# State-space scan stage of a fused layer: order of the tiles, second norm, softplus and diagonals

## The reference

```
z   = LN(x)                       zn = LN(z) * norm_w + norm_b
p   = zn @ x_proj_w.T             split into rank part r (128), B (64 states), C (64 states)
dt  = softplus(r @ dt_proj_w.T + dt_proj_b)
h_n[t] = exp(-exp(A_log[n]) * dt[t]) * h_n[t-1] + dt[t] * zn[t] * B_n[t]     for 64 states n
y[t]   = sum_n C_n[t] * h_n[t]  +  D_param * z[t]
x  += y @ out_proj_w.T
```

## Time and profile before

| | us |
|---|---|
| three runs | 678.47, 679.4, 685.2 |
| median | 679.4 |
| the profiled execution, its time | 682.74 |
| its span, first to last instruction | 680.9 |
| VectorE busy, whole span | 498.0 |
| scan stage, first statistics to the last sum | 36.19 to 169.03 |
| first scan starts, last scan starts | 67.99, 159.16 |
| mean of one scan, of one product with C | 2.285, 2.756 |
| mean granted clock of TensorE | 0.927 |

### The profile page before, as it was taken

How to read it: one execution, slowest core, us unless ns; L and a number is a source line. 1 busy time by engine, 2 the same in 40 slices (tenths; PEclk the granted TensorE clock), 3 DMA queues, 4 the chain that set the end, 5 groups by cost and what they waited for, 6 DMA issues and landing times. The chain is left out here.

```text
span 680.9 us, 12861 instructions
## 1 busy us (share of the span) xinstructions
PE 583.0 (86%) x4813; PEld 395.7 (58%) x4813; DVE 498.0 (73%) x852; ACT 396.1 (58%) x750; POOL 335.5 (49%) x265
## 2 busy tenths in 40 slices
PE   4976899997899999799953878878788988889997
PEld 3542355444677777587730555545455575668886
DVE  4357999996678885479966999999999945433322
ACT  4226975552435554456775999999899943421111
POOL 1009999996204442244605898998878830000000
PEclk9987999999999999999975898897887769999999
DMA  9526600000927664046547788897859638900000
GB/s 354 237 74 252 247 0 1 0 1 0 310 83 238 212 210 140 17 127 176 149 130 161 147 141 172 156 175 155 162 132 159 122 64 337 398 1 1 0 1 15
DMA packets 97090, 92.90 MB, mean 136 GB/s; under 512 B 70595, under 2 KB 88323, under 8 KB 93638
## 3 DMA queue, kind: packets, MB, share of 16 engines
q1 hardware_dynamic: 93760, 90.46, 47.9%
q10 hardware_dynamic: 3270, 1.65, 0.8%
HBM read 68.59 MB, written 6.62 MB: 110 GB/s over the span
## 5 line engine op out<-in xcount | busy, mean ns | idle before, releaser
L2150 DVE TENSOR_REDUCE d_nmax<-d_psum 128x1 f32<-128x1024 f32 x128 | 151.5, 1212 | 5.2 <-PE d_psum L2306 5.2
L2306 PE MATMUL d_psum<-kst,qT 96*128 96x512 bf16 x256 | 90.7, 452 | 38.2 <-ACT d_e L2247 15.7
L528 POOL TENSOR_TENSOR b_h<-b_h,b_cb 128x1024 f32<-128x1024 f32 x32 | 88.2, 2756 | 6.3 <-DVE b_h L578 4.5
L2247 ACT ACTIVATE d_e<-d_psum,d_nmax 128x1024 f32<-128x1024 f32 x64 | 71.3, 1115 | 14.9 <-DVE d_nmax L2150 14.4
L2130 POOL TENSOR_SCALAR d_rounded<-d_e,d_lift 128x1024 f16<-128x1024 f32 x64 | 72.1, 1127 | 13.8 <-issue 6.8
L2130 POOL TENSOR_SCALAR d_rounded<-spare,d_lift 128x1024 f16<-128x1024 f32 x62 | 70.4, 1135 | 16.0 <-ACT d_lift L2251 11.8
L578 DVE TENSOR_TENSOR_SCAN b_h<-b_dA,b_psum 128x1024 f32<-128x1024 f32 x32 | 73.1, 2285 | 2.5 <-ACT b_dA L633 2.0
L633 ACT ACTIVATE b_dA<-b_dtT,b_A 128x248 f32<-128x248 f32 x128 | 53.7, 490 | 33.1 <-DVE b_h L578 28.1
L2247 ACT ACTIVATE spare<-d_psum,d_nmax 128x1024 f32<-128x1024 f32 x64 | 71.4, 1122 | 1.9 <-DVE d_nmax L2150 1.9
L689 PE MATMUL b_psum<-b_bdiag,b_dtx 128*128 128x512 f32 x128 | 60.2, 594 | 0.8 <-DVE b_h L578 0.8
L2333 PEld LDWEIGHTS d_psum<-d_ident_f,d_rounded 128*128 128x128 f16 x512 | 40.8, 115 | 32.5 <-issue 18.9
(11 more groups left out here) (439 smaller groups left out, 1189.3 us busy)
## 6 DMA issues: line engine op xcount, KB each, us to landing
c_w<-in_w0gu SPq DMA_DIRECT2D x16, 768.0 KB, 4.8
kst<-kT_scratch SPq DMA_DIRECT2D x84, 128.0 KB, 2.7
w<-in_w SPq DMA_DIRECT2D x5, 1920.0 KB, 21.3
b_cb<-c_scratch SPq DMA_DIRECT2D x4, 2048.0 KB, 7.1
c_w<-in_w0dn SPq DMA_DIRECT2D x16, 384.0 KB, 5.6
kT_scratch<-k_kT SPq DMA_DIRECT2D x12, 384.0 KB, 3.7
a_ctx<-in_ctx SPq DMA_DIRECT2D x2, 2048.0 KB, 18.8
k_ctxT<-in_ctxT SPq DMA_DIRECT2D x12, 256.0 KB, 3.1
```

Source lines behind the costliest of these rows:

```text
L528: nc.gpsimd.tensor_tensor(hv, hv, cv, ALU.mult).then_inc(hc_ready, 1)
L2150: nc.vector.tensor_reduce(nm[:, t, m:m + 1, f:f + 1], quarter(m, j).unsqueeze(1), AX.X, ALU.max, negate=True).then_inc(nm_ready, 1)
L2247: nc.scalar.activation(e[j].unsqueeze(1), quarter(m, j).unsqueeze(1), ACT.Exp, bias=nm[:, t, m:m + 1, f], accum_out=zp[:, t, m:m + 1, f]). ...
L2306: last = nc.tensor.matmul(quarter(m, j)[:, b * 512:(b + 1) * 512], qT[0:QROWS, m:m + 1, t * P:(t + 1) * P], kst[m % 2][0:QROWS, at:at + 51 ...
```

## The change

- Norms: `LayerNorm` is split into `moments` and `inverse`. The second norm's variance is worked out from the first's: var(z) = var(x) * rstd * rstd. zn is written from x directly with the product of both factors, and z after it, with a semaphore of its own.
- TensorE transposes zn alone and signals, then z; the 13 fillers there are gone. VectorE makes znT first, without waiting between the halves, and zDT after it.
- Softplus: Exp is written to SBUF, Ln takes 1 + e in its own pass, the relu part runs before Exp is waited for, and the lost part of 1 + e is added as a polynomial in four operations. The reciprocal, the comparison and three products are gone. The 20 fillers become 13, and they run behind the transposes of C.
- dtxT, its transposes and dtx go by channel halves.
- The decays of tiles 0 and 1 wait for dt alone.
- Tiles: for the first 8 groups the halves alternate (m = 2n + c), then groups 8 to 15 of half 0, then those of half 1.
- Diagonals: GpSimd makes those of 20 states, 4 an instruction; ScalarE 88, 4 ahead of the decays and 4 behind the decays of each tile.

```
@@ -81,19 +81,8 @@
...
-        for t in range(TC):
-            last = nc.vector.bn_stats(self.stats[:, t, :], in_[:, t, :])
-        step(last)
-        for t in range(TC):
-            last = nc.vector.bn_aggr(self.mv[:, t, :], self.stats[:, t, :])
-        step(last)
-        nc.vector.tensor_scalar(self.ve[:, :], self.mv[:, :, 1], LN_EPS, None, ALU.add).then_inc(self.var_ready, 1)
-        dve.wait_ge(self.std_ready, 1)
-        step(nc.vector.reciprocal(self.rstd[:, :], self.std[:, :]))
-
-        step(nc.vector.scalar_tensor_tensor(self.std[:, :], self.ve[:, :], -0.5, self.rstd[:, :], ALU.mult, ALU.mult))
-        step(nc.vector.tensor_tensor(self.std[:, :], self.std[:, :], self.rstd[:, :], ALU.mult))
-        step(nc.vector.scalar_tensor_tensor(self.rstd[:, :], self.std[:, :], 1.5, self.rstd[:, :], ALU.add, ALU.mult))
+        self.moments(step, in_)
+        self.inverse(dve, step, self.mv[:, :, 1])
...
@@ -105,6 +94,27 @@
...
+    def moments(self, step, in_):
+
+        nc = self.nc
+        for t in range(TC):
+            last = nc.vector.bn_stats(self.stats[:, t, :], in_[:, t, :])
+        step(last)
+        for t in range(TC):
+            last = nc.vector.bn_aggr(self.mv[:, t, :], self.stats[:, t, :])
+        step(last)
+
+    def inverse(self, dve, step, var):
+
+        nc = self.nc
+        nc.vector.tensor_scalar(self.ve[:, :], var, LN_EPS, None, ALU.add).then_inc(self.var_ready, 1)
+        dve.wait_ge(self.std_ready, 1)
+        step(nc.vector.reciprocal(self.rstd[:, :], self.std[:, :]))
+
+        step(nc.vector.scalar_tensor_tensor(self.std[:, :], self.ve[:, :], -0.5, self.rstd[:, :], ALU.mult, ALU.mult))
+        step(nc.vector.tensor_tensor(self.std[:, :], self.std[:, :], self.rstd[:, :], ALU.mult))
+        step(nc.vector.scalar_tensor_tensor(self.rstd[:, :], self.std[:, :], 1.5, self.rstd[:, :], ALU.add, ALU.mult))
...
@@ -407,9 +417,13 @@
...
-    CHUNK = 2 * NT
-    POOLED = 10 * NT
-    SPARE = 3
+    CHUNK = NT
+    POOLED = 5 * NT
+    SPARE = 4
+    TOGETHER = 8
+    ORDER = [(c, n) for n in range(TOGETHER) for c in range(DCH)] \
+        + [(c, n) for c in range(DCH) for n in range(TOGETHER, TILES)]
+    ENDS = ORDER.index((0, TILES - 1))
...
@@ -431,16 +445,20 @@
...
-        sp_relu, sp_z, sp_r, sp_q = (h[s][:, q * DCH * T:(q + 1) * DCH * T].rearrange("p (c t) -> p c t", c=DCH)
-                                     for s in range(2) for q in range(2))
+        sp_relu, sp_lost, sp_e = (h[q // 2][:, q % 2 * DCH * T:(q % 2 + 1) * DCH * T].rearrange("p (c t) -> p c t", c=DCH)
+                                              for q in range(3))
...
-        sp_e, sp_l, sp_u, sp_d = (ps[:, b, :].rearrange("p (c t) -> p c t", c=DCH) for b in range(4))
+        sp_d, sp_l, sp_c = (ps[:, b, :].rearrange("p (c t) -> p c t", c=DCH) for b in range(3))
+        var_z = sb("b_var_z", [P, TC])
+        scale_zn = sb("b_scale_zn", [P, TC])
...
@@ -451,8 +469,8 @@
...
         def tiles_of(body):
 
-            for m in range(DCH * TILES):
-                body(m // TILES, m % TILES, m, m % UN)
+            for m, (c, n) in enumerate(ORDER):
+                body(c, n, m, m % UN)
...
@@ -531,43 +549,49 @@
...
-                lnA.vector(dve, step, z, x)
-                lnB.vector(dve, step, zn, z)
-                nc.vector.tensor_copy(lnA.std[:, :], lnB.rstd[:, :]).then_inc(zn_ready, 1)
+                lnA.moments(step, x)
+                lnA.inverse(dve, step, lnA.mv[:, :, 1])
+                step(nc.vector.tensor_tensor(var_z[:, :], lnA.mv[:, :, 1], lnA.rstd[:, :], ALU.mult))
+                step(nc.vector.tensor_tensor(var_z[:, :], var_z[:, :], lnA.rstd[:, :], ALU.mult))
+                lnB.inverse(dve, step, var_z[:, :])
+                step(nc.vector.tensor_tensor(scale_zn[:, :], lnA.rstd[:, :], lnB.rstd[:, :], ALU.mult))
+                for out, by, ready in ((zn, scale_zn, zn_ready), (z, lnA.rstd, z_ready)):
+                    for t in range(TC):
+                        nc.vector.tensor_scalar(out[:, t, :], x[:, t, :], lnA.mv[:, t, 0:1], by[:, t:t + 1], ALU.subtract,
+                                                ALU.mult).then_inc(ready, 1)
                 dve.wait_ge(w_in, 80)
+                dve.wait_ge(znT_psum, 1)
+                for k in range(KC):
+                    nc.vector.tensor_scalar(znT[:, k, :], ps[:, 0, k * T:(k + 1) * T], cols[:, 0, k:k + 1],
+                                            cols[:, 1, k:k + 1], ALU.mult, ALU.add).then_inc(znT_ready, 1)
                 dve.wait_ge(zT_psum, 1)
                 for k in range(KC):
-                    step(nc.vector.tensor_scalar(znT[:, k, :], ps[:, 0, k * T:(k + 1) * T], cols[:, 0, k:k + 1],
-                                                 cols[:, 1, k:k + 1], ALU.mult, ALU.add))
                     step(nc.vector.tensor_scalar(zDT[:, k, :], ps[:, 1, k * T:(k + 1) * T], cols[:, 3, k:k + 1],
                                                  None, ALU.mult))
-                nc.vector.tensor_copy(lnA.std[:, :], lnB.rstd[:, :]).then_inc(znT_ready, 1)
...
                 nc.vector.tensor_copy(cT[:, :], ps[0:N, 5, 0:T]).then_inc(cT_ready, 1)
-                dve.wait_ge(spe_ready, DCH)
-                nc.vector.tensor_scalar(sp_u, sp_e, 1.0, None, ALU.add).then_inc(spu_ready, 1)
-                step(nc.vector.tensor_scalar(sp_d, sp_e, 1.0, 1.0, ALU.add, ALU.subtract))
-                step(nc.vector.tensor_scalar(sp_z, sp_d, 0.0, None, ALU.is_equal))
...
-                step(nc.vector.reciprocal(sp_r, sp_d))
+                dve.wait_ge(spa_ready, DCH)
                 for k in range(DCH):
                     step(nc.vector.tensor_scalar(sp_relu[:, k, :], ps[:, 4, k * T:(k + 1) * T], cols[:, 2, k:k + 1], 0.0,
                                                  ALU.add, ALU.max))
+                dve.wait_ge(spe_ready, DCH)
+                step(nc.vector.tensor_scalar(sp_d, sp_e, 1.0, 1.0, ALU.add, ALU.subtract))
+                step(nc.vector.tensor_tensor(sp_lost, sp_e, sp_d, ALU.subtract))
+                step(nc.vector.scalar_tensor_tensor(sp_c, sp_d, -2.0, sp_lost, ALU.add, ALU.mult))
+                step(nc.vector.scalar_tensor_tensor(sp_relu, sp_c, -0.5, sp_relu, ALU.mult, ALU.add))
                 dve.wait_ge(spl_ready, 1)
-                step(nc.vector.tensor_tensor(sp_d, sp_l, sp_r, ALU.mult))
-                step(nc.vector.tensor_tensor(sp_q, sp_d, sp_z, ALU.add))
-                step(nc.vector.tensor_tensor(sp_d, sp_e, sp_q, ALU.mult))
-                nc.vector.tensor_tensor(dtT[:, :, :], sp_d, sp_relu, ALU.add).then_inc(dt_ready, 1)
+                nc.vector.tensor_tensor(dtT[:, :, :], sp_l, sp_relu, ALU.add).then_inc(dt_ready, 1)
                 dve.wait_ge(dt_ready, 1)
-                nc.vector.tensor_tensor(dtxT[:, :, :], dtT[:, :, :], znT[:, :, :], ALU.mult).then_inc(dtxT_ready, 1)
-                dve.wait_ge(dtx_psum, 1)
-                nc.vector.tensor_copy(dtx[:, :, :], ps[:, 6, :].rearrange("p (t c) -> p t c", t=TC)).then_inc(dtx_ready, 1)
-
-
-                dve.wait_ge(dtx_ready, 1)
+                for c in range(DCH):
+                    nc.vector.tensor_tensor(dtxT[:, c, :], dtT[:, c, :], znT[:, c, :], ALU.mult).then_inc(dtxT_ready, 1)
+                for c in range(DCH):
+                    dve.wait_ge(dtx_psum, c + 1)
+                    nc.vector.tensor_copy(dtx[:, :, c * P:(c + 1) * P], ps[:, 6 + c, 0:T].rearrange("p (t c) -> p t c", t=TC))\
+                      .then_inc(dtx_ready, 1)
+                dve.wait_ge(dtx_ready, DCH)
                 nc.vector.tensor_copy(lnA.std[:, :], lnB.rstd[:, :]).then_inc(h_ready, UN)
...
@@ -606,12 +630,13 @@
...
                 for k in range(DCH):
-                    astep(nc.scalar.activation(sp_l[:, k, :], ps[:, 4, k * T:(k + 1) * T], ACT.Abs,
-                                               bias=cols[:, 2, k:k + 1]))
+                    nc.scalar.activation(sp_l[:, k, :], ps[:, 4, k * T:(k + 1) * T], ACT.Abs,
+                                         bias=cols[:, 2, k:k + 1]).then_inc(spa_ready, 1)
+                act.wait_ge(spa_ready, DCH)
                 for k in range(DCH):
                     nc.scalar.activation(sp_e[:, k, :], sp_l[:, k, :], ACT.Exp, scale=-1.0).then_inc(spe_ready, 1)
-                act.wait_ge(spu_ready, 1)
-                nc.scalar.activation(sp_l, sp_u, ACT.Ln).then_inc(spl_ready, 1)
+                act.wait_ge(spe_ready, DCH)
+                nc.scalar.activation(sp_l, sp_e, ACT.Ln, bias=1.0).then_inc(spl_ready, 1)
                 act.preload_act_table(ACT.Exp)
...
@@ -619,14 +644,15 @@
...
-                first = 2 * TC * NT
+                first = 4
...
                 def decay(c, n, m, s):
-                    act.wait_ge(h_ready, m + (UN - 1))
+                    if m >= 2:
+                        act.wait_ge(h_ready, m + (UN - 1))
...
                     for at in late[first + m * SPARE:first + (m + 1) * SPARE]:
                         diagonal(*at)
```

(28 more changed lines are left out.)

9 lines of the change are left out of this document (5 added, 4 removed).

## The result

| | before | after |
|---|---|---|
| median of 20 runs each | 682.53 us | 677.6 us |
| ratio after to before | | 0.9934 (0.9915 to 0.9953) |
| profiled execution, span | 682.74, 680.9 | 679.14, 677.3 |
| mean granted clock | 0.927 | 0.909 |

The change gains 4.9 us, 0.7%. The forecast was 670 with a range from 665 to 675.5. The measured time lies outside it: of the 9.9 us of its sum 4.9 arrived.

The account below looks back on a forecast made before the run. VectorE bounds the scan at 2.94 us per tile, and the serial chain ahead shifts everything. Gains 5.07 + 6.2 + 0.3 less 1.7 for the clock give 9.9 us; from the middle reading, 681.1, that gives 671.2; stated 670, range 665 to 675.5.

Parts of the forecast that it names:

- Norms and transposes: From the first norm's inverse deviation to drT: projection and drT start 5.07 us earlier, 1.85 of it from late fillers.
- Softplus: From drT's start to dt ready: 7.22 us in place of 13.45, a gain of 6.2 us.
- Scan pitch in the steady part: Tiles stay 2.94 us apart, set by VectorE; ScalarE's four diagonals per tile take 1.29 and fit.
- rival 3: Scan tiles: ScalarE becomes the bound with four diagonals, 3.24 us against 2.94 for 21 tiles; 675.8 us, chance 0.08.
- Rival 2: Clock low in more places, doubling the projection and dt matmuls: gain 7.0 us, 672.4 us, chance 0.14.
- Rival 5: Slower: first scan tiles at half clock, each low tile costing 2.7 us; 8 give 689.4 us, chance 0.03.
- rival 1: Before the first scan: no clock fall, or one ending before TensorE has work; gain 11.6 us, 667.8 us, chance 0.15.
- dt to the first scan: From dt ready to scan 0: gain 0.3 us (0 to 0.8), with dtxT's two halves priced at 0.92 together.
- Scan. Alternating halves changes no tile's work: Scan tiles: VectorE keeps 2.94 us per tile, no drive waits for a diagonal; priced at nothing.
- The clock's price: TensorE idles 3 us before dtxT, its clock falls for 3.41 us at half speed: 1.7 us lost (0 to 3.4).
- a half of dtxT over 0.9 (the lock): Sign of being wrong: VectorE and GpSimd lock each other out of SBUF at dtxT; priced up to 1.9 us worse.
- an end that comes earlier by less than the first scan does: Sign of being wrong: the kernel's end gains less than the first scan, forecast 9.9 to 11.6 us earlier.

Follow-up runs that it names:

- l: The kernel before with only the softplus changed (Abs, Exp and Ln on ScalarE, no reciprocal): 688.25 us, ratio to before 1.0075.
- m: k with the norms, transposes and their 13 fillers as before: 675.38 us, ratio to before 0.9878.
- a: The change, with GpSimd's second product with C made to wait for VectorE's first half sum: 678.43 us, ratio to before 0.9922.
- e: The change plus an unread 0.40 us copy on VectorE between scans 0 and 1: 674.89 us, ratio to before 0.9883.
- r: The change plus only k's filler matmuls in TensorE's waits at the stage's end: 679.09 us, ratio to before 0.9926.
- b: The change with 28 filler matmuls in place of 13 behind the transposes of C: 680.35 us, ratio to before 0.9948.
- c: The change, with GpSimd pausing its diagonals until both halves of dtxT are written: 677.22 us, ratio to before 0.9903.
- d: The change with the edits of a, b and c together: 675.99 us, ratio to before 0.9901.
- k: f plus 13 more filler matmuls in TensorE's waits at the stage's end: 670.37 us, ratio to before 0.9806, the fastest kernel.
- h: The kernel before with only the norms and transposes changed, without the 13 fillers behind them: 683.27 us, ratio to before 1.0008.
- f: The change with the edits of e, b and c together: 674.44 us, ratio to before 0.9874.
- g: The change with the tile order and the split of the diagonals as before: 684.67 us, ratio to before 1.0028.
- o: k with tile order and diagonals as before, and without GpSimd's pause: 680.82 us, ratio to before 0.9956.
- i: The kernel before with 56 fillers, started without waiting for ScalarE, in place of the softplus's 20: 683.76 us, ratio to before 0.9991.
- q: i plus k's filler matmuls at the stage's end: 681.82 us, ratio to before 0.9984.

## Why the prediction was wrong

**Norms and transposes: right for the trace it was read from.** drT starts 4.90 earlier, forecast 5.07. Of that, 1.7 is the fall of the clock in the fillers, which l and m did not have, so some executions have only 3.2 to gain. **Softplus: right.** From drT to dt 7.20 us, forecast 7.22; gain 6.25 against 6.2. **Scan pitch in the steady part: right**, 2.95 with four diagonals, which take 1.26 (forecast 1.29): rival 3 is out. Rival 2 is out, since the clock did not fall in the projection. Rival 5 priced low tiles rightly in kind, but only tiles 1 to 3 met one, and rival 1 didn't occur.

**Two steps failed: "dt to the first scan", and "Scan. Alternating halves changes no tile's work", a term put at nothing.** The change, a, e and r have the same code up to scan 0, so they are four executions of the first step; b, c and d take its causes away. Times are in us:

| | lock on dtxT | low stretch between dt and scan 0 | dt to scan 0 | half sum blocked, low stretch behind it | scan 0 to scan 4 |
|---|---|---|---|---|---|
| before | barely (0.92) | none | 4.61 | no, none | 11.41 |
| the change | yes | 6.83 | 8.03 | yes, 6.83 | 16.19 |
| r | yes | 3.41 | 6.70 | yes, 3.41 | 15.03 |
| a | yes | 3.41 | 6.93 | yes, none | 13.82 |
| e | yes | 3.41 | 6.76 | no, none | 11.41 |
| b | yes | none | 5.24 | yes, 3.41 | 15.00 |
| c | no | 3.41 | 5.60 | yes, none | 13.37 |
| d | no | none | 3.91 | yes, 3.41 | 15.18 |

From dt to scan 0 the forecast was 1.4 us more than before (1.7 for the clock less 0.3). It was 2.1 to 2.3 more in three executions and 3.4 in the profiled one of the change.
- dtxT's halves at 0.92 together were 2.10. I took the value from a row in which GpSimd was the one lengthened. The lock rule stood in the text, priced at up to 1.9, and did not enter the sum. Runs: b against d, full clock with and without the lock, 5.24 against 3.91, 1.3 us.
- The clock's price was right in kind and size: one stretch of 3.41 costs 1.7 without the lock (c against d) and 1.5 to 1.7 with it (r, e and a against b). In the profiled execution of the change the stretch was 6.83 and cost 2.8. That much is the luck of one execution.
- The gain put at 0.3 was 0.7 (d against before).

**What the prediction did not have at all** is the half sum of tile 0. It looked at what each instruction costs in the steady part and not at which of two engines starts first when the tiles begin. Before, the start was staggered: scan 1 came 2.45 us after scan 0, since ScalarE's decays were late. The change made the decays early, scans 0 and 1 ran back to back (4.46 for two), and GpSimd's second product got in 0.08 us ahead of the half sum. That costs 2.13. It can also take the clock down: in the change scan 3 waited another 2.80, 4.9 together, the 4.8 us lost in four tiles. In a and c nothing fell and the four tiles lost 2.4 and 2.0; in b, d and r they lost 3.6 to 3.8. Run e takes all of it away with a copy of 0.40 us.

With r's values the change keeps 11.15 - 2.09 - 3.62 = 5.4 us, near the 4.9 of the runs.

**The level.** Before's median over 20 runs is 682.5, not the 681.1 that the forecast was taken from, and 670 is 1.2 below its own middle, without a reason given. These 2.6 us are part of the 7.6 between 670 and 677.6, and have nothing to do with the mechanism.

Two of the prediction's own signs came: "a half of dtxT over 0.9 (the lock)", with 0.92 and 1.26, and "an end that comes earlier by less than the first scan does"; but no rival stood for the second. With both places mended and the tail filled, k comes to 670.4 and the stage is 11.9 us shorter. That it equals the forecast 670 is partly luck: the tail's fillers were no part of the change.

**Open:** why h's 4.9 us at scan 0, of which 2.9 are left at the stage's end, don't show in twelve runs, why f shows so little over e, and why the tail's fillers bring 4 us behind f and nothing behind the change. One profiled execution each, with low stretches in other places each time, can't settle it.

## What to carry to other kernels

When a chain in front of a pipelined loop gets shorter, look at the loop's first turns as a timetable: which engine's instruction starts first at each shared resource, and what that was before. A row's duration taken where one engine won such a meeting is not the price where it loses; price the loser. When a stall appears on an engine that isn't at work, check next what TensorE's clock does behind it, since the loss there can be as large as the stall itself: here from nothing (c) to 2.80 (the change) behind a stall of 2.13. And look at more than one execution before a fall of the clock is priced: kernels with the same code up to a place had it or not, 3.41 or 6.83 long.

## What the hardware showed unexpectedly

- A VectorE sum of two SBUF inputs that takes 0.69 us took 2.81 or 2.82 in nine kernels (the change, a, b, c, d, g, l, o, r) when GpSimd's 2.35 us product had started just before; when VectorE was first by 0.04 us, in before, it took 0.69 and the product 2.87. In every pair of these traces the one that started second paid.
- A copy of 2 columns, b_lnA_std from b_lnB_rstd, took 1.71 us in l and 0.61 in the change beside GpSimd's diagonals, 0.17 in k, where it started 0.02 ahead of one of them.
- Low stretches of the granted clock that began in the scan stage or just behind it were 3.41, 6.83, 10.24 or 13.65 us long, in all traces that had one; later stages also had some of 17 to 31 us.
- TensorE idle for 2.31 us ahead of the same transposes: the clock fell in before, i and q and not in l and m. The same fillers took 4.66 or 2.97 us.
- Four 128-column diagonals in a row on ScalarE take 1.26 us, 0.32 each, though one counts 0.38.
